# Two adaptive-norm layers with routed low-rank feed-forward: where GpSimd waits for the next x tile, and where SyncE issues its load

## What is computed

```python
x = x + L0_ffn(L0_cond(x, cond))      # per sample: a 32x32 mix of the channels, weights from cond, plus a bias
x = x + L1_ffn(L1_cond(x, cond))      # grouped convolution, 9 taps, along the 512 columns, plus ctx and bias
# L0_ffn(y): y @ W_up.T + lora_B[e] @ (lora_A[e] @ y), e = argmax of 4 gate logits of each row
# L1_ffn(c): c @ W_base.T + b_base + 2 of 8 rank-16 experts, weighted by a softmax over the gate
```

## Time and profile before

| | us |
|---|---|
| median of 3 runs (407.73 to 410.41) | 408.29 |
| the profiled execution, as timed | 406.51 |
| its span, first to last instruction | 404.7 |
| PE busy in the span (88%) | 356.3 |
| PEld busy (85%) | 342.7 |
| DVE busy (59%) | 237.6 |
| POOL busy (50%) | 200.5 |
| ACT busy (33%) | 135.3 |

### The profile page before, as it was taken

One profiled execution on the slowest core, in us unless ns is written; L12 is line 12 of the kernel. 1 busy time (PEld: TensorE's weight loads), 2 busy tenths in 40 slices (PEclk: granted clock), 3 DMA queues, 4 the chain that ended last, 5 costly groups with the idle time before them and its releaser, 6 DMA issues.

```text
span 404.7 us, 9092 instructions
## 1 busy us (share of the span) xinstructions
PE 356.3 (88%) x2593; PEld 342.7 (85%) x2593; DVE 237.6 (59%) x977; ACT 135.3 (33%) x410; POOL 200.5 (50%) x229
## 2 busy tenths in 40 slices
PE   2878998689999999999998989898998999999985
PEld 1666998689998988898998989888998889898984
DVE  2667576256565655556566565556666565555654
ACT  2544333123333333332333333332333333333331
POOL 8476455424554455444455455444455455544540
PEclk9998999899999999999999999999999999999999
DMA  7524367333323223333322323333322323333221
GB/s 169 174 69 114 66 162 143 68 81 78 55 50 71 70 66 78 78 78 78 78 39 63 73 64 74 78 78 78 78 43 59 72 67 72 78 78 78 55 53 53
DMA packets 54301, 31.98 MB, mean 79 GB/s; under 512 B 43868, under 2 KB 44300, under 8 KB 54288
## 3 DMA queue, kind: packets, MB, share of 16 engines
q1 hardware_dynamic: 40064, 27.69, 28.7%
q10 hardware_dynamic: 13984, 3.73, 6.6%
q0 software_dynamic: 240, 0.41, 0.4%
HBM read 14.35 MB, written 8.93 MB: 58 GB/s over the span
## 4 chain that ended last, share of the span: by engine, by line
SPq 22%; DMA 21%; PE 15%; DVE 13%; issue 11%; POOL 6%; ACT 2%; ACTq 1%; DVEq 1%; POOLq 1%
SPq L294 21%; DMA xt<-in_x 18%; PE ps_mix L939 5%; POOL xq_lo L454 5%; DVE ps_ct L752 5%; PE ps_conv L939 4%; DVE x1s L725 4%; DMA xq<-x1s 2%; PE ps_up L917 2%; DVE zT L732 2%; ACTq L294 1%; DMA mix_all<-agg_mix 1%; PE ps_up L922 1%; SPq L301 1%; PE ps_base L1078 1%
## 5 line engine op out<-in xcount | busy, mean ns | idle before, releaser
L473 POOL TENSOR_TENSOR y_lo<-y,y_hi 128x512 fp32r<-128x512 f32 x31 | 40.0, 1291 | 102.5 <-ACT y_hi L527 102.5
L454 POOL TENSOR_TENSOR xq_lo<-xq,xq_hi 128x260 fp32r<-128x260 f32 x64 | 45.8, 735 | 82.4 <-DMA xt<-in_x 75.4
L1078 PE MATMUL ps_base<-base_hi,c_hi 128*128 128x392 f32 (+1 forms) x256 | 78.2, 322 | 1.8 <-ACT c_hi L573 1.3
L917 PE MATMUL ps_up<-up_hi,y_hi 128*128 128x292 f32 (+1 forms) x256 | 71.8, 304 | 4.6 <-DMA mix_all<-agg_mix 4.6
L1078 PE MATMUL ps_base<-base_lo,c_hi 128*128 128x392 f32 (+1 forms) x256 | 75.3, 311 | 0.0
L917 PE MATMUL ps_up<-up_lo,y_hi 128*128 128x292 f32 (+1 forms) x256 | 69.5, 293 | 0.0
L461 POOL TENSOR_TENSOR x1b<-x1s,bbase_s 128x256 f32<-128x256 f32 x64 | 57.7, 930 | 0.0
L917 PEld LDWEIGHTS ps_up<-up_hi,y_hi 128*128 128x128 f32 x256 | 49.0, 191 | 5.5 <-issue 5.5
L1078 PEld LDWEIGHTS ps_base<-base_hi,c_hi 128*128 128x128 f32 x256 | 48.2, 188 | 2.3 <-DVE ot L760 2.2
L917 PEld LDWEIGHTS ps_up<-up_lo,y_hi 128*128 128x128 f32 x256 | 49.1, 192 | 0.0
L1083 PE MATMUL ps_base<-base_hi,c_lo 128*128 128x392 f32 (+1 forms) x256 | 48.4, 311 | 0.0
(11 more groups left out here) (178 smaller groups left out, 669.9 us busy)
## 6 DMA issues: line engine op xcount, KB each, us to landing
xt<-in_x SPq DMA_DIRECT2D x32, 256.0 KB, 2.8
out_x<-ot SPq DMA_DIRECT2D x32, 256.0 KB, 2.7
xq<-x1s SPq DMA_DIRECT2D x160, 32.5 KB, 2.1
xq<-x1s ACTq DMA_DIRECT2D x96, 32.5 KB, 2.2
rows<-agg_rows SPq DMA_DIRECT2D x2, 597.0 KB, 5.0
wbase_raw<-in_L_ffn_W_base SPq DMA_DIRECT2D x2, 512.0 KB, 4.2
rows<-agg_rows SPq DMA_DIRECT2D x1, 598.0 KB, 4.4
wup_raw<-in_L_ffn_W_up ACTq DMA_DIRECT2D x2, 256.0 KB, 4.6
```

The source lines that it names most:

```text
L454: pool.tensor_tensor(xq_lo[:, gp], xq[:, gp], xq_hi[:, gp], ALU.subtract)\
L473: pool.tensor_tensor(y_lo[:], y32[:], y_hi[:], ALU.subtract).then_inc(ylo_done, 1)
L917: pe.matmul(into, y_hi[:, k], w[:, k, cols], start=(k == 0 and w is up_hi), stop=False, skip_group_check=True)
L1078: pe.matmul(ps_base[:, j, 0:width], c_hi[:, q], w[:, q, j, 0:width], start=(q == 0 and w is base_hi), stop=False, skip_group_check=True)
```

## The change

Two edits, in the body functions of SP and of GpSimd. Everything else of the program is as before; line numbers behind the edits are two higher.

```diff
 @block.sync body(i, par)
                 if once(i):
 
+                    if not isinstance(i, int) or i + 2 < NT:
+                        if isinstance(i, int) and i == 0:
+                            sp.wait_ge(xtp_done, 1)
+                        sp.wait_ge(ylo_done, i + 1)
+                        load_x(i + 2, par)
                     sp.wait_ge(x1_done, 2 * (i + 1))
                     for gp in range(GP):
                         for b in range(SPT // 2 + gp):
                             move_x(sp, gp, b)
-
-                    if not isinstance(i, int) or i + 2 < NT:
-                        load_x(i + 2, par)
 @block.gpsimd body(i, par)
                 if once(i - 1):
 
-                    if once(i + 1):
-                        pool.wait_ge(x_in[1 - par], (i + par) * 8 + 16)
                     for gp in range(GP):
                         pool.wait_ge(xqhi_done, 2 * i - 1 + gp)
                         pool.wait_ge(xq_in[gp], i * XQ)
                         pool.tensor_tensor(xq_lo[:, gp], xq[:, gp], xq_hi[:, gp], ALU.subtract)\
                             .then_inc(xqlo_done, 1)
                     if isinstance(i, int) and i == 1:
                         pool.wait_ge(in_rows, 32)
+                    if once(i + 1):
+                        pool.wait_ge(x_in[1 - par], (i + par) * 8 + 16)
                     pool.wait_ge(x1_done, 2 * i)
```

## The result

| | before | after |
|---|---|---|
| median of the runs, us | 408.01 (4 runs, 406.51 to 410.41) | 374.22 (4 runs, 372.55 to 377.20) |
| the profiled execution, as timed | 406.51 | 375.63 |
| its span | 404.7 | 373.8 |
| PE busy in it | 356.3 (88%) | 352.3 (94%) |

The ratio is 0.9175, with a 95% interval of 0.9094 to 0.9256: faster. Two later sets of the same kernel had medians of 376.05 and 376.0 us (ratios 0.9215 and 0.9204), so 374 to 376 is its time. The forecast was 377 for the median and 374.9 for the profiled execution, which took 375.63. The three sets of runs put the gain at 33.8, 33.0 and 31.8 us, the two profiles at 30.9; 31.6 was forecast.

A forecast was written before the change was run, and what follows sets the result against it. The prediction took PE's wait for `xq_lo`, held up by GpSimd's wait for the load of x, as the bound. Terms 31.0 + 0.6 = 31.6 us, from 408.29 to 376.7, rounded to 377; range 373 to 386.

The forecast's parts named there:

- The bound: Loop tiles: PE waits for `xq_lo`, held by GpSimd's wait for x; without it TensorE bounds at 10.10 to 10.24 us.
- The stall, 31.0 us: PE's wait for `xq_lo` in 28 tiles goes whole, saving 31.0 us; bounds 23.4 to 34.2.
- The order on SP: In loop tiles the store goes out 0.8 us earlier, the x load at about 211.1; load issue costs 0.
- rival A: `xq_lo` of group 1 becomes late through later-landing `x1` moves; 389 us at 1.2 us later; chance 0.12.
- the room: Loop tiles: `xq_lo` of group 1 ends 0.76 us before an unstalled PE wants it.
- The landings: Two 256 KB transfers still follow the moves, landings alike at 2.7 and 2.8 us; effect on the moves' landing counted 0.
- Body 3, 0.6 us: Load no longer stands between moves and `mix_all`, shortening PE's 4.56 us wait: 0.6 us saved, bounds 0 to 3.4.
- The sign given for body 4: PE's wait for `mix_all` in body 4 would be about 4 us.
- The first bodies: Bodies 0 to 2: loads move ahead of set-up transfers; counted 0, bounds 1 us either way.
- Rival B: No change: GpSimd's wait for x only moves, delaying `x1b`, `order_x` and `y_lo`; time stays at 408; chance 0.03.
- Rival C: Slower: TensorE without its pause per tile is granted less clock; 448 us at clock 0.80; chance 0.04.
- Contention: GpSimd and DVE could disturb each other as `xq_lo` and `x1b` move; at most 0.05 us, counted 0.

The follow-up runs named there:

- the long delay: Changed kernel with two extra full-size GpSimd subtractions into a scratch tile ahead of each `xq_lo` of group 1: 396.43 us.
- the last version: Changed kernel with the last two `mix_all` transfers issued at the top of SP's body 3, ahead of the x load and the `x1` wait: 370.64 us, ratio 0.9077.
- the short delay: Changed kernel with one extra half-size GpSimd subtraction into a scratch tile ahead of each `xq_lo` of group 1: 377.83 us.

## Why the prediction was right

**The bound.** That the chain over SP's moves, the load of x and `xq_lo` made the tile, and not the 88% busy TensorE, is shown from both sides: about 0.5 us of PE work a tile left out of the kernel before gave nothing, and left out of the changed one gave 0.50 a tile; and moving the wait alone or the load alone took the tile from 11.32 to 10.22.

**The stall, 31.0 us.** It went whole. The two early tiles and the 28 behind body 4 gave 1.52 + 29.23 = 30.75. The weight loads' idle with its correction was the right row, and the matmuls' 23.4, kept as the low bound, was 7 too low. The tile length of 10.10 to 10.24 came out at 10.22.

**The order on SP.** The store went out 3.74 behind the first move instead of 4.37, so 0.6 us earlier, where 0.8 was forecast. The load went out 4.73 behind it, and not at 4.2: in the tile shown `y_lo` ends at 217.51 and the load is issued 0.62 us later, which I had counted as nothing (in about half of the tiles it is 0.2). It costs nothing. The five moves and the way to `xq_hi` of group 1 stayed as they were: 218.47 - 213.40 = 5.07, against 5.06. So rival A had nothing to stand on, and the room, forecast at 0.76, is 0.76 in the tile shown (0.83 to 0.87 in every other one) and about 0.77 by the long delay.

**The landings** of x and of the store even became shorter, 2.6 and 2.0 us for 2.8 and 2.7; no wait for either stands in the list of waits.

**Body 3, 0.6 us.** This term was too small: 1.48 in the table of marks, with the wait for `mix_all` down from 4.56 to 3.13. I took the difference of issue, which measured 0.63 as forecast, and left the landing at nothing, "nearest to the row". The landing got 0.8 shorter in these two profiles (5.13 to 4.33), and 0.7 to 1.2 over all profiles. What failed is the choice of the landing's value at the end of its range. The sign given for body 4, a wait for `mix_all` of about 4 us, missed with it: it is 3.1 to 3.55. What the prediction did not have at all is the low clock behind this wait, in both kernels, which the last version shows to be worth 1.5 to 2 us in the changed one.

**The first bodies, counted at 0, bounds of 1.** The first mark came 1.33 later, outside the bound. But the change is not what moved it: in other profiles it stands at 41.58 with SP and GpSimd as in the kernel before, and at 39.70 with them as in the changed one. It goes with the clock of that stretch; see below. The other terms gave 30.75 + 1.48 = 32.2, which is 0.6 more than forecast; with this 1.33 the span lost 30.9, which is 0.7 less. That the profiled execution came so near to its 374.9 is in part two errors of opposite sign, the landing and the scatter of the set-up.

**Rival B**, no change, is not only unlikely but settled: GpSimd's wait for x at its new place was 0.3 us a tile even with the load left late. **Rival C**, less clock: the granted clock is 1.00 over 276 us in which PE never pauses. The Trainium skill, TensorE: Matmul & The Clock Gate, Part 1, says that one busy core does not trip the peak-current limiter; the trace agrees with its 1.00. **Contention** of GpSimd with DVE: `xq_lo` went from a median of 734 to 745 ns,

```profile
L454 POOL TENSOR_TENSOR xq_lo<-xq,xq_hi x64: 731/745/754, 38.6 to 361.6; 128x260 fp32r<-128x260 f32 x64
```

which is 11 ns more, in the direction in which the GPSIMD Engine Reference of the Trainium skill, Specifications, points, and far inside the room. But `x1b`, which moved too, went the other way, from a median of 942 ns to 908, so that this case does not show contention to have grown.

## What to carry to other kernels

Ask of each wait whether the instruction behind it uses what is waited for; in a list that runs in order, a wait one step too early holds up work that needs nothing of it, and a load one step too late does the same from the other side, so that either repair is enough. When an engine is 88% busy and the waits name something else, leave a known amount of its work out of the kernel: if the time stays, that work was not in the way. And price the gain with a tile of the same trace that happens not to have the wait, after measuring how early the next thing in line is.

## What the hardware showed beyond what was expected

The same PE idle time is followed by full clock in one execution and by half in another. PE waits 2.5 us for `base_p` near 28 us in the kernel before as in the changed one, and from 30 to 34 us the granted clock is 1.00, 2.4 GHz, in the first and 0.50, 1.2 GHz, in the second. The end of the wait and the clock, before:

```profile
27.74 1.09 PE L877 MATMUL ps_base<-ident,base_p 128*128 128x128 f32 x8 [2.49 <-POOL base_p L423]
...
30.00:34.00 4.00, 2.66 (x22) 2.36 (x22) 3.23 (x7) 1.09 (x3) 3.43 (x5) 1.00 0.13 18
```

After:

```profile
27.67 1.24 PE L879 MATMUL ps_base<-ident,base_p 128*128 128x128 f32 x8 [2.48 <-POOL base_p L425]
...
30.00:34.00 4.00, 3.32 (x15) 2.89 (x14) 1.32 (x4) 1.24 (x3) 3.36 (x4) 0.50 0.24 68
```

It is not the change. In five of the twelve profiles the clock was low for part or all of the stretch from 28 to 34 us, and two of the five are of variants of the kernel before (the wait alone, and the one with less PE work, which is left out behind this stretch). Seven had 1.00, the third profile of the changed kernel among them. Nor is it the length of the pause: it is 2.5 us in eleven of them, and 3.35 in the twelfth (the short delay), which kept 1.00. The five with the low clock reach the first mark at 40.83 to 41.58 us, the seven others at 39.70 to 40.57, on average 1.1 us earlier. So a set-up phase with pauses gives times that scatter by a microsecond or more, and a profile should be compared stage by stage before a small difference is put down to an edit. What decides between the two is not shown here.
